# Relation messages of a graph network: summed by target after a message stage, or added by indirect DMA onto one array of sums in DRAM while the messages are made

## The reference

```python
seg = edge_type * n + dst
agg = jax.ops.segment_sum(x[src], seg, num_segments=N_REL * n)
cnt = jax.ops.segment_sum(ones, seg, num_segments=N_REL * n)
mean = agg.reshape(N_REL, n, -1) / jnp.maximum(cnt, 1.0).reshape(N_REL, n, 1)
h1 = jnp.einsum('rni,rio->no', mean, W_rel) + x @ W_root + b_rgcn
xw = h1 @ W_gcn
...
out = jax.ops.segment_sum(xw[src] * norm[:, None], dst, num_segments=n)
out = out + xw * (dinv * dinv)[:, None]
```

## Time and profile before

| | |
|---|---|
| median of 3 runs | 3945.08 us (3943.74 to 3946.80) |
| span of the profiled execution | 3937.5 us |
| what lies around the span (median less span) | 7.6 us |
| PE busy | 3619.1 us, 92% |
| DVE, ACT, POOL busy | 1958.2 us, 1683.3 us, 1555.4 us |
| mean granted TensorE clock | 0.971 |
| relation stage, first to last product | 2160.2 to 3475.4 us of the span |
| sum stage, up to the first transposes of `conv3` | 3475.4 to 3746.2 us |

### The profile page before, as it was taken

One profiled execution on the slowest core, in us unless ns is written; L12 is line 12 of the kernel. 1 busy time (PEld: TensorE's weight loads), 2 busy tenths in 40 slices (PEclk: granted clock), 3 DMA queues, 4 the chain that ended last, 5 costly groups with the idle time before them and its releaser, 6 DMA issues.

```text
span 3937.5 us, 58219 instructions
## 1 busy us (share of the span) xinstructions
PE 3619.1 (92%) x18463; PEld 2965.8 (75%) x18473; DVE 1958.2 (50%) x2783; ACT 1683.3 (43%) x2911; POOL 1555.4 (40%) x1168
## 2 busy tenths in 40 slices
PE   8998868999988897589989999999999999989998
PEld 4555437999978897333335999999999999965588
DVE  7245788888533635899955333332233331013334
ACT  1113677888832321499981333333333333300021
POOL 3887886666600101000001444444444444357600
PEclk9999998999989998799999999999999999999999
DMA  4343212232232302311014555555555553368901
GB/s 144 90 125 74 46 20 63 74 95 74 78 115 90 123 28 81 108 50 40 34 50 144 198 184 184 173 177 186 184 184 189 179 170 133 112 237 302 284 22 67
DMA packets 176460, 483.10 MB, mean 123 GB/s; under 512 B 40798, under 2 KB 57205, under 8 KB 176342
## 3 DMA queue, kind: packets, MB, share of 16 engines
q1 hardware_dynamic: 87414, 201.95, 15.7%
q0 software_dynamic: 54368, 185.24, 15.2%
q10 hardware_dynamic: 34560, 94.45, 6.8%
HBM read 357.64 MB, written 123.55 MB: 122 GB/s over the span
## 4 chain that ended last, share of the span: by engine, by line
PE 40%; ACT 7%; POOL 5%; issue 3%; DVE 2%; DMA 1%; SPq 0%; POOLq 0%; DVEq 0%; ACTq 0%
PE ps L1898 30%; POOL work L1979 5%; ACT work L1279 4%; PE ps L1886 3%; ACT ps L1270 3%; PE ps L1562 3%; PE ps L306 2%; PE ps L298 1%; DVE work L1101 1%; PE ps L1216 1%; DVE work L1129 0%; ACT work L1289 0%; DMA ct<-x_d 0%; DMA work<-msg_d,ct 0%; PE ps L324 0%
## 5 line engine op out<-in xcount | busy, mean ns | idle before, releaser
L1898 PE MATMUL ps<-wsplit,xsplit 128*128 x6840 | 1238.3, 337 | 2.7 <-DVEq L1838 2.7
L1898 PEld LDWEIGHTS ps<-wsplit,xsplit 128*128 128x128 f32 x6840 | 1182.9, 188 | 2.9 <-issue 2.9
L1835 DVE CAST wsplit<-wplain 128x768 fp32r<-128x768 f32 x204 | 117.3, 575 | 760.8 <-PE ps L1898 745.4
L1865 POOL TENSOR_TENSOR xsplit<-ct,xsplit 128x768 fp32r<-128x768 f32 x190 | 369.3, 1944 | 296.2 <-ACTq L1930 296.2
L1279 ACT ACTIVATE work<-ps,work 128x418 f32<-128x418 f32 x720 | 438.6, 632 | 108.5 <-PE ps L1189 103.2
L1935 ACT ACTIVATE ct<-ps,invs 128x768 f32<-128x768 f32 x190 | 171.5, 902 | 714.3 <-PE ps L1898 714.3
L1226 PE MATMUL ps<-hbuf,work 128*128 128x193 f32 x2400 | 455.8, 328 | 14.8 <-DVE work L1143 13.1
L1226 PEld LDWEIGHTS ps<-hbuf,work 128*128 128x128 f32 x2400 | 408.0, 190 | 42.8 <-issue 16.9
L1270 ACT ACTIVATE ps<-work,lr 128x418 f32<-128x418 f32 x720 | 431.8, 634 | 6.0 <-DMA work<-lrow_d 6.0
L1129 DVE SCALAR_TENSOR_TENSOR work<-work,cnt 128x1250 f32<-128x1250 f32 x240 | 350.0, 1459 | 133.5 <-ACT work L1279 132.8
L1860 POOL DMA_INDIRECT ct<-x_d,relrec x190 | 201.1, 1059 | 457.8 <-PE ps L1886 450.2
(11 more groups left out here) (212 smaller groups left out, 4380.5 us busy)
## 6 DMA issues: line engine op xcount, KB each, us to landing
wplain<-in_L_gnn_W_rel SPq DMA_DIRECT2D x34, 2304.0 KB, 9.7
msg_d<-ct ACTq DMA_DIRECT2D x190, 384.0 KB, 2.6
work<-lrow_d SPq DMA_DIRECT2D x47, 625.0 KB, 3.7
feat_d<-work ACTq DMA_DIRECT2D x30, 386.0 KB, 4.1
hbuf<-feat_d SPq DMA_DIRECT2D x60, 193.0 KB, 2.5
gat_d<-work POOLq DMA_DIRECT2D x12, 960.0 KB, 5.2
xplain<-gat_d SPq DMA_DIRECT2D x30, 384.0 KB, 3.1
work<-xa_d SPq DMA_DIRECT2D x27, 384.0 KB, 3.3
```

Source lines behind the costliest of these rows:

```text
L1865: g.tensor_tensor(xlo7[:, k % XW, :], xt7[:, k % 2].rearrange("p c n -> p (c n)"), xhi7[:, k % XW, :].bitcast(F32), ALU.subtract).then_inc ...
L1898: last = pe.matmul(ps[:, 4 + 2 * (u % 2) + h, 0:HALF], x[:, u, c * P:(c + 1) * P], w[:, bass.ds(base + (c * D + h * HALF), HALF)], start=( ...
```

## The change

The message store, the second list's use in the sum stage, and the sum stage itself are gone. The sums live in DRAM (`acc_d`): POOL stores the ten tiles of `hbuf` there, and each message tile is added by an indirect DMA with addition, whose start waits until the one before has landed. Within one such DMA a row may appear once only, so messages of one tile with equal keys (target and relation) are summed first: the six transposes become products of the gathered rows with a 128 x 128 matrix of equal keys, made by POOL (`equal`), and all but the last edge of a key are sent to rows of `acc_d` that nobody reads. These targets are worked out beforehand, in the W_OUT stage, by POOL (`pool_same`) and DVE (`dve_target`), four tiles to a batch, from the keys turned into rows in DRAM (`pe_keys`, `act_keys`). SP loads the sums back at the end; the weights of the last convolution are loaded and split as if they were a 35th relation. In the first phase the target list's places come first, and the records have three numbers instead of four and two.

```diff
         def pe_rel(pe):
...
+                pe.wait_ge(s_same7, k + 1)
...
-                    last = pe.transpose(ps[:, 2 * (u % 2) + c // 3, (c % 3) * P:(c % 3 + 1) * P], rows7[:, u % GW, 0, c * P:(c + 1) * P], ident[:, :])
+                    last = pe.matmul(ps[:, 2 * (u % 2) + c // 3, (c % 3) * P:(c % 3 + 1) * P], rows7[:, u % GW, 0, c * P:(c + 1) * P],
+                                     same7[u % GW], start=True, stop=True)
...
         def pool_rel(g, step):
...
+            def equal(k):
+                b, w = divmod(k, KB)
+                if w == 0:
+                    g.wait_ge(s_keyin[b % 2], 16 * (b // 2 + 1))
+                if k >= GW:
+                    g.wait_ge(s_turn7, k - GW + 1)
+                g.tensor_scalar(same7[k % GW], key_rows[:, b % 2, w * P:(w + 1) * P], keys[:, k:k + 1], None, ALU.is_equal).then_inc(s_same7, 1)
+
+            def add(k):
+                g.wait_ge(s_msg7, k + 1)
+                if k:
+                    g.wait_ge(s_msgst[(k - 1) % 2], 16 * ((k - 1) // 2 + 1))
+                g.indirect_dma_start(out=acc_d, out_offset=bass.IndirectOffsetOnAxis(relrec[:, REC * k + 2:REC * k + 3], 0),
+                                     in_=msg7[:, k % 2, :], in_offset=None, compute_op=ALU.add).then_inc(s_msgst[k % 2], 16)
...
             for k in range(GW):
                 gather(k)
+            for k in range(2):
+                equal(k)
+            for j in range(NT):
+                g.wait_ge(W_ROOT.emptied, W_ROOT.b["emptied"] + j + 3)
+                g.dma_start(acc_d[j * P:(j + 1) * P, :], hbuf[:, j * D:(j + 1) * D]).then_inc(s_acc0, 16)
+            g.wait_ge(s_acc0, 16 * NT)
             for k in range(RT):
                 if k + GW < RT:
                     gather(k + GW)
+                if k + 2 < RT:
+                    equal(k + 2)
+                if k >= 3:
+                    add(k - 3)
                 low(k)
+            for k in range(RT - 3, RT):
+                add(k)
...
         def sp_rel(sp):
...
+            sp.wait_ge(s_split7, R + 1)
+            sp.dma_start(w, a["L3_gnn_W_gcn"].rearrange("(c p) n -> p c n", p=P)).then_inc(s_wrel, 16)
+            for u in range(2):
+                sp.wait_ge(s_msgst[u], 16 * (RT // 2))
+            for j in range(NT):
+                sp.dma_start(hbuf[:, j * D:(j + 1) * D], acc_d[j * P:(j + 1) * P, :]).then_inc(s_sums[SUM_PARTS[j]], 16)
...
         def act_rel(act, step):
...
-                act.dma_start(msg_d[bass.ds(k * P, P), :], msg7[:, u % 2, :]).then_inc(s_msgst[u % 2], 16)
+                act.sem_inc(s_msg7, 1)
+            def key_rows_in(b, u):
+                act.wait_ge(s_same7, KB * b - KB)
+                act.dma_start(key_rows[:, u, :], key_batch(b)).then_inc(s_keyin[u], 16)
...
+        def pool_same(g, step):
+            def load(b):
+                g.dma_start(key_rows[:, b % 2, :], key_batch(b)).then_inc(s_keyin0[b % 2], 16)
+            step(g.tensor_copy(keys, rel3[:, :, 1]))
+            g.wait_ge(s_keyst, 32)
+            load(0)
+            for b in range(KEY_BATCHES):
+                k0, k1 = batch(b)
+                if b:
+                    g.wait_ge(s_later, b)
+                if k1 < RT:
+                    load(b + 1)
+                g.wait_ge(s_keyin0[b % 2], 16 * (b // 2 + 1))
+                for w in range(k1 - k0):
+                    step.count(g.tensor_scalar(same0[:, w, :], key_rows[:, b % 2, w * P:(w + 1) * P], keys[:, k0 + w:k0 + w + 1], None, ALU.is_equal))
+                step.wait()
+                found = same0[:, 0:k1 - k0, :]
+                g.tensor_tensor(found, found, tri[:, :].unsqueeze(1).to_broadcast([P, k1 - k0, P]), ALU.mult).then_inc(s_same0, 1)
+
+        def dve_target(v, step, b):
+            k0, k1 = batch(b)
+            later, target = small[:, 48:48 + k1 - k0], rel3[:, k0:k1, 2]
+            v.wait_ge(s_same0, b + 1)
+            step(v.tensor_reduce(later, same0[:, 0:k1 - k0, :], AX, ALU.max))
+            v.sem_inc(s_later, 1)
+            step(v.scalar_tensor_tensor(target, later, dummy_row, target, ALU.mult, ALU.max))
+
+        TARGETS = {(l, j): 3 if j < 6 else 2 for l in range(2) for j in range(NT) if l or j}
...
         def dve_wout(v, step):
...
+                    for b in TARGET_OF.get((l, j), ()):
+                        dve_target(v, step, b)
...
         def pool_wout(g, step):
+            pool_same(g, step)
             g.wait_ge(s_split4, 3 * KC)
```

More of the change, by code:

```diff
@@ L604, in pe_phase1, with prefixes @@
             pe.wait_ge(s_const, 2)
+            def prefixes(n, b0, nb):
+                pe.wait_ge(s_rowsum, n + 1)
+                pe.matmul(ps[:, 4 + 2 * n, b0:b0 + nb], tri[0:EP, :], small[0:EP, b0:b0 + nb], start=True, stop=True)
+                pe.matmul(ps[:, 5 + 2 * n, b0:b0 + nb], ones[0:EP, :], small[0:EP, b0:b0 + nb], start=True, stop=True).then_inc(s_offs, 1)
             def offsets(j, behind):
[L608 to L611, removed]
+                if j == 2 and behind:
+                    prefixes(1, 0, R)
+            prefixes(0, R, NT)
             W_AH.multiply_single(pe, offsets)
-            pe.wait_ge(s_offtaken, 1)
+            pe.wait_ge(s_offtaken, 2)
             for s in W_H[0:2]:
@@ L1314, in build @@
                          [(gat_d[l], h) for l in range(3) for h in range(4)], False)
-        assert att0.used <= WORK - KC * D
-        s_invs = sem("inverse_counts_gathered")
+        assert att0.used <= WORK - KC * D - RT - 2
+        keys0 = work[:, 4 * KC * D - RT - 2:4 * KC * D]
+        keys = lr[:, 0:RT + 2]
+        key_turned = xplain[:, 4 * D:4 * D + P].bitcast(U16)
+        key_rows = drec[:, 0:KB * P].bitcast(U16).rearrange("p (u n) -> p u n", u=2)
+        s_keys, s_keyt, s_keyst = (sem(n) for n in ("keys_ready", "keys_turned", "key_rows_stored"))
@@ new lines, in build, with pe_keys, act_keys @@
+        s_keyin = [sem(f"key_rows_in{u}") for u in range(2)]
+        s_invs = sem("inverse_counts_gathered")
+        def pe_keys(pe):
+            pe.wait_ge(s_keys, 1)
+            pe.transpose(ps[:, 0, HALF:HALF + P], keys0[:, 0:P], ident[:, :])
+            pe.transpose(ps[0:RT + 2 - P, 1, HALF:HALF + P], keys0[:, P:RT + 2], ident[:, :]).then_inc(s_keyt, 1)
+        def act_keys(act, step):
+            act.wait_ge(s_keyt, 1)
+            step.count(act.activation(key_turned[:, 0:P], ps[:, 0, HALF:HALF + P], ACT.Copy))
+            step(act.activation(key_turned[0:RT + 2 - P, P:2 * P], ps[0:RT + 2 - P, 1, HALF:HALF + P], ACT.Copy))
+            act.dma_start(keyrow_d[0:P, :], key_turned[:, 0:P]).then_inc(s_keyst, 16)
+            act.dma_start(keyrow_d[P:RT + 2, :], key_turned[0:RT + 2 - P, P:2 * P]).then_inc(s_keyst, 16)
@@ L1320, in gather_inverses @@
+        for place, count in TARGETS.items():
+            TARGET_OF[place] = range(at, min(at + count, KEY_BATCHES))
+            at += count
+        assert at >= KEY_BATCHES
         def gather_inverses(g, first, last):
@@ L1814, in build, with sums_whole @@
         s_split7 = sem("weights_split7")
+        s_same7, s_msg7, s_acc0 = sem("equal_keys7"), sem("messages_ready7"), sem("first_sums_stored")
+        s_sums = [sem(f"sums_in{u}") for u in range(3)]
+        SUM_PARTS = [0] + [1] * 4 + [2] * (NT - 5)
+        def sums_whole(j):
+            return s_sums[SUM_PARTS[j]], 16 * SUM_PARTS.count(SUM_PARTS[j])
         def sp_rel(sp):
@@ L1854, in dve_rel @@
             relation(R - 1, 1)
+            relation(R, 0)
+            v.sem_inc(conv3.s_w, KC)
         def pool_rel(g, step):
@@ L1917, in act_rel @@
         def act_rel(act, step):
+            for b in range(2):
+                act.dma_start(key_rows[:, b, :], key_batch(b)).then_inc(s_keyin[b], 16)
             act_root(act)
@@ L1933, in store @@
                 act.wait_ge(s_prod7, k + 3)
[L1934 removed]
+                if stores is not None:
+                    act.wait_ge(s_msgst[u % 2], 16 * stores)
                 step(act.activation(halves(msg7[:, u % 2, :]), ps[:, 4 + 2 * (u % 2):6 + 2 * (u % 2), 0:HALF], ACT.Copy,
@@ L1984, in pe_sum @@
-        def pe_sum(pe):
-            def group(k, u, gathers):
-                pe.wait_ge(s_sel8, k + 1)
-                if not isinstance(k, int) or k >= 2:
-                    pe.wait_ge(s_add8, k - 1)
-                for w in range(GT):
-                    pe.wait_ge(s_g8[GT * u + w], 16 * gathers)
-                    for h in range(2):
-                        last = pe.matmul(ps[:, 2 * (u % 2) + h, 0:HALF], sel8[:, GT * (u % 2) + w, :],
-                                         mg8[:, GT * u + w, h * HALF:(h + 1) * HALF], start=(w == 0), stop=(w == GT - 1))
-                last.then_inc(s_sum8, 1)
-            for k in range(UP):
-                group(k, k, 1)
-            with pe.Fori(0, BG // UP - 1) as i:
-                for u in range(UP):
-                    group(UP * i + UP + u, u, i + 2)
-            for k in range(BG // UP * UP, BG):
-                group(k, k % UP, k // UP + 1)
@@ L2059, in _ @@
```

(2 more changed lines are left out.)

222 lines of the change are left out of this document (105 added, 117 removed).

## The result

The changed kernel takes 3979.1 us (median, 3978.0 to 3980.8), the kernel before 3944.4 us in the same series: a ratio of 1.0091, 95% interval 1.0077 to 1.0105. The forecast was 78 us faster; it is 35 us slower. The profiled execution has a span of 3976.4 us against 3937.5 us, 38.9 us more, and the traces are compared on that.

The account below looks back on a forecast made before the run. The prediction took PE's work in its stages, and PE's waits where they meet, as the bound. Its terms -258 + 126 + 0 + 51 + 3 = -78 took 3945.1 to 3867 us, range 3800 to 4120.

Parts of the forecast that it names:

- Sum stage, -258: Between last message and last convolution: 284.4 us replaced by last add, loads and first tile, 26 us; -258 us.
- Float32 products, +126: Relation stage, PE: twelve records of 0.109 us replace six transposes, 0.66 us more a tile, 190 tiles; +126 us.
- Rival D: Float32 products of 128 columns take 0.195 us though the clock is full: +322 in place of +126, 4063 us; chance 0.05.
- Adds, 0: Relation stage: chained adds cost 0 if one lands within 7.4 us; 6.7 us taken, so PE sets the pace.
- the sign that was to show it: Relation stage: POOL's wait ahead of the add would be for the message (ACT), not for the landing.
- one late add of 10 us is made good by the next ones: Relation stage: low part made two tiles ahead, gather four, so a 10 us add is recovered by later adds.
- Targets, +51: W_OUT stage: 48 batches of 3.9 us chained through POOL and DVE, 187 us against a 132.6 us window; +51 us.
- The upper end, 5.6 us and +135: W_OUT stage: with the full 1.94 us for the product and twice the compares, a batch is 5.6 us; +135 us.
- The shared interface: W_OUT stage: POOL and DVE contend for SBUF, a batch meeting such a DVE instruction is 0.96 us later; 48 us.
- rival C: W_OUT stage: shared SBUF interface adds 48 us, or a batch is 5.6 us; 3915 to 3951 us, chance 0.08.
- The rest, 0: First phase's earlier target records and key turning in the W_OUT stage: 0 us; the latter +4 if uncovered.
- Start of the relation stage, +3: POOL stores ten start tiles and waits before its first low part; 2162.2 to 2164 against 2160.24; +3 us.

Follow-up runs that it names:

- the run with transposes: Changed kernel with PE turning gathered rows by transposes again in place of float32 products, POOL still making the marks: 3948.3 us.
- the run without marks: Changed kernel with transposes again and POOL making no marks of equal keys in the relation stage: 3872.7 us, ratio 0.9817.

## Why the prediction was wrong, by its own steps

From the forecast (-78) to the measured spans (+38.9) are 117 us: 103 lie in the targets, 11 in the first phase and some 3 in all the rest.

- *Sum stage, -258:* right, -260. Tile 1's products start 24.0 us behind the last message's scaling (3795.65 - 3771.63), where 26 was forecast. The path was right, and tile 0's products took 7.36 us where 9.25 was taken.
- *Float32 products, +126:* right, +124: 1.34 us for 12 records in every tile, where 1.31 was taken. Rival D is out.
- *Adds, 0:* right in the time, with less to spare than the text says. The landing was sized well (median 5.7 us, at the most 11.1; 5.9 and 10.1 were taken), and so was POOL's own work in a tile: the adds come every (3772.9 - 2344.6) / 189 = 7.56 us, and its idle time ahead of adds and gathers is (228.2 + 155.3) / 190 = 2.02 us, which leaves 5.54; 5.5 was taken. That agreement is luck: the items listed there add up to 4.66 unless each of the four has its 0.3 us of gap behind it, and the add's record is 1.77 us where 1.06 was taken, the marks 0.85 where 0.3 was; what made up for both is that records overlap where gaps were expected (last section). But the sign that was to show it, a wait for the message and not for the landing, failed: of POOL's waits ahead of the adds 178.6 us were for the landing and 24.4 for ACT, while PE had no gap. And the step "one late add of 10 us is made good by the next ones" holds only slowly: with PE free to go at 6.92 us the adds come every 7.41, so at 7.59 they had less than 0.2 us a tile left. Taking the marks from POOL won 0.36 of the 0.49 back, so how fast a late add is made good depends on POOL's other work too. The late adds are those beside weight loads, as the prediction had it: in the changed kernel the 67 under way beside one land in 6.6 us (median, at the most 11.1), the other 123 in at most 6.6.
- *Targets, +51:* this is the step that failed, by the size of one row of its sum. The mechanism was right, down to the chain through one buffer and what stands behind DVE's wait. "Four compares of 128 columns (0.29 each, from the select of that size)" are 0.59 each alone and 0.705 on average; from the first reduction at 1156.13 to the last at 1437.6 the 48 batches took 281.5 / 47 = 5.99 us each in place of 3.9. Of these 2.1 us, 1.66 are the compares (4 x 0.705 - 1.16), 0.07 the load's issue, -0.09 the product, 0.05 the reduction, and 0.4 the hand-overs with what DVE does for its tile between them. 48 x 5.99 = 287 us in a window of 133 leave +150 after the 4 us made before; +154 was measured. The upper end, 5.6 us and +135, had the compares right (twice 0.29) and no contention; its terms add up to 5.7, and it came near 5.99 in part by luck, for it charged 1.94 us for a product that took 1.21. It was named as an end and got too little of the chance.
- *The shared interface,* priced only in rival C: it is there, and smaller than its 48 us. A compare takes 0.59 us (median) and up to 1.92. The slow ones are those beside DVE's low parts and splits: the ten beside a low part alone took 1.46 us on average, most of those beside splits 1.3 to 1.7, the ten beside an eviction alone 0.59. At 0.705 on average against 0.594 in the median that is 190 x 0.11 = 21 us. The Trainium skill's rule (page "GPSIMD Engine Reference", section "Key points") that GpSimd and VectorE contend for SBUF when a DVE instruction has two SBUF inputs or runs in a two-port mode agrees with these rows: the low part L410 reads two arrays in SBUF, the eviction L1542 reads one (`hbuf`) and the product (`ps`). Rival C gave its two causes as one or the other; both came, the compares with some 60 us and the contention with 21.
- *The rest, 0:* the second failure. The text followed the moved prefix sums to the engine that uses their result, DVE (0.22 us of wait), and not to the one on which two instructions were put ahead of everything, PE: +11 us.
- *Start of the relation stage, +3:* from the root stage's first block (+169.3) to the first products (+172.2) it is +2.9. The path differs in its last step: PE waited 3.37 us at 2329.83 for the marks of the third tile, not for a low part. The other 4.5 of the +7.3 arose between the convolution and the root stage. They are scatter of single executions rather than the change: that stretch takes 618.2 us in the kernel before and 622.7 in the changed one, but also 622.8 in the run with transposes and 618.7 in the run without marks, whose code up to there is the changed kernel's.

With the two measured sizes in its sum the forecast gives -258 + 126 + 154 + 3 + 11 = +36, and +38.9 was measured.

## What to carry to other kernels

A wait in the middle of an in-order queue costs its length times the number of rounds, so the price of the slowest instruction in the loop decides: take it from a row with the same operation and operand types, or let the range carry twice the nearest one. When an engine is to share a stage with another, look at which instructions of the two lie side by side: here the low parts slowed the compares, the evictions did not. When two small instructions move, look at what they now stand in front of on their own engine, not only at who needs their result. And when an engine waits for another in the same loop, ask first whether one of them can do the whole loop: here DVE alone needs 2.26 us for what the two did in 5.4 to 6.

## What the runs showed of the hardware that was not expected

- A compare of 128 columns (16-bit keys in, bf16 out) with one scalar for each partition is 0.59 us on POOL; on DVE compare and mask together are 1.13 / 4 = 0.28 us.
- An indirect add of 128 rows of 3 KB lands in 5.7 us (median) where a gather of the same bytes lands in 4.1 beside it. The forecast took 1.2 us more for reading the old sums; the difference is 1.6, and no run shows what it consists of.
- POOL's record of the low part grew from 1.94 us to 2.36 without the work being longer: it starts 1.1 us after the start of an add of 1.6 us, so the two records overlap by the difference:

```profile
2659.17 1.60 POOL L2005 DMA_INDIRECT acc_d<-ct,relrec  x1 [4.39 <-DMA acc_d<-ct,relrec]
2660.28 2.38 POOL L1986 TENSOR_TENSOR xsplit<-ct,xsplit 128x768 fp32r<-128x768 f32 x1
```

From the end of the add's record this low part takes 1.89 us; the first ones of the stage, which have no add ahead, took 1.82 to 1.85. The sum of the records is not POOL's time; the distance of two adds less the idle time is.
